# Delta stage in tiles of 64 tokens of two sequences, 64x64 blocks, and the decays in one matmul per eight heads

## The reference

```python
qkvz = x @ W_in                      # 128 -> 4 * 1024
b, a = jnp.split(x @ W_ba, 2, axis=-1)
qkv = silu(causal_conv_of_4_taps(qkv, conv_w))   # every channel for itself
beta = jax.nn.sigmoid(b)
g = -A * jax.nn.softplus(a + dt_bias)
q = _l2norm(q) * HD ** (-0.5)
k = _l2norm(k)
def step(S, inp):                    # over the tokens of one sequence
    qt, kt, vt, gt, bt = inp
    S = S * jnp.exp(gt)[..., None, None]
    pred = jnp.einsum('bhk,bhkv->bhv', kt, S)
    S = S + jnp.einsum('bhk,bhv->bhkv', kt, (vt - pred) * bt[..., None])
    o = jnp.einsum('bhk,bhkv->bhv', qt, S)
    return (S, o)
...
y = y * jax.lax.rsqrt(jnp.mean(y * y, axis=-1, keepdims=True) + 1e-06)
y = norm_w * y * jax.nn.silu(z)
return y.reshape(Bb, Tt, KV) @ W_o
```

## Time and profile before

| | |
|---|---|
| median of 3 runs | 6675.69 us (6673.12, 6675.69, 6717.01) |
| span of the profiled execution | 6691.0 us |
| delta loop, 16 turns | some 3890 us of it, from 125 us to some 4020 us |
| one tile, t = 0 and 2 / 1 / 3 | 57.7 / 62.5 / 64.5 us |
| busy over the span | PE 5879.5, DVE 3696.7, ACT 3292.2, POOL 2549.1 us |

### The profile page before, as it was taken

One profiled execution on the slowest core, in us unless ns is written; L12 is line 12 of the kernel. 1 busy time (PEld: TensorE's weight loads), 2 busy tenths in 40 slices (PEclk: granted clock), 3 DMA queues, 4 the chain that ended last, 5 costly groups with the idle time before them and its releaser, 6 DMA issues. The chain is left out here.

```text
span 6691.0 us, 188335 instructions
## 1 busy us (share of the span) xinstructions
PE 5879.5 (88%) x67493; PEld 4461.9 (67%) x67494; DVE 3696.7 (55%) x7182; ACT 3292.2 (49%) x7191; POOL 2549.1 (38%) x2432
## 2 busy tenths in 40 slices
PE   5999999999999999999999997668888799995586
PEld 4777777777777777777777775556666566664486
DVE  5555555555555555555555555654444466665443
ACT  2555555555555555555555552242333345552165
POOL 5545444544454545454544453340000200003553
PEclk9999999999999999999999997888898899996598
DMA  3000000000000000000000001020000000001124
GB/s 96 21 22 19 18 22 22 18 19 22 21 19 19 21 22 19 19 21 22 19 18 22 22 18 32 28 77 1 1 1 0 3 0 0 0 0 40 38 62 123
DMA packets 99365, 161.44 MB, mean 24 GB/s; under 512 B 19973, under 2 KB 82245, under 8 KB 96069
## 3 DMA queue, kind: packets, MB, share of 16 engines
q1 hardware_dynamic: 76260, 121.44, 6.0%
q0 software_dynamic: 14080, 26.64, 1.2%
q10 hardware_dynamic: 8320, 4.19, 0.2%
HBM read 118.03 MB, written 104.87 MB: 33 GB/s over the span
## 5 line engine op out<-in xcount | busy, mean ns | idle before, releaser
L802 PE MATMUL bank<-wc,hT 128*128 128x512 f32 (+1 forms) x2344 | 1077.6, 571 | 47.6 <-issue 29.0
L972 PE MATMUL bank<-X,kqe 128*128 128x64 f32 x6240 | 775.4, 278 | 42.1 <-DVE rb L1472 19.7
L972 PEld LDWEIGHTS bank<-X,kqe 128*128 128x128 f32 x6240 | 727.5, 192 | 84.1 <-DVE rb L1472 55.1
L1210 ACT ACTIVATE TT<-bank 128x512 bf16<-128x512 f32 x640 | 381.8, 597 | 612.8 <-PE bank L953 612.8
L1512 DVE TENSOR_TENSOR yb<-bank,masks 128x512 bf16<-128x512 f32 x768 | 526.5, 687 | 137.1 <-PE bank L935 135.8
L802 PEld LDWEIGHTS bank<-wc,hT 128*128 128x128 f32 x2344 | 391.0, 191 | 310.5 <-issue 282.2
L1310 POOL TENSOR_TENSOR qa<-qa,qt 128x512 f32<-128x512 f32 x390 | 487.4, 1271 | 34.8 <-POOL qt L1305 34.8
L1451 DVE TENSOR_TENSOR kqe<-bank,ex 128x512 f32<-128x512 f32 x520 | 335.1, 686 | 273.8 <-PE bank L879 273.8
L1210 ACT ACTIVATE T<-bank 128x512 bf16<-128x512 f32 x640 | 349.5, 595 | 272.1 <-PE bank L946 270.2
L1343 POOL TENSOR_SCALAR_AFFINE_SELECT kqe<-kqe 128x512 f32<-128x512 f32 x260 | 215.7, 830 | 641.0 <-DVE kqe L1451 640.9
L1305 POOL TENSOR_TENSOR qt<-qp,cq 128x512 f32<-128x512 f32 x390 | 400.4, 1048 | 28.0 <-POOL qa L1310 28.0
(11 more groups left out here) (536 smaller groups left out, 13459.3 us busy)
## 6 DMA issues: line engine op xcount, KB each, us to landing
sent_l0f<-blank_l0f SPq DMA_DIRECT2D x64, 528.0 KB
sent_l1m<-blank_l1m SPq DMA_DIRECT2D x64, 528.0 KB
xin<-sent_l1m SPq DMA_DIRECT2D x139, 66.0 KB
taken_l1m<-back_l1m SPq DMA_DIRECT2D x16, 512.0 KB, 8.7
xin<-sent_l0f SPq DMA_DIRECT2D x75, 66.0 KB
decay_sums<-decay_rows SPq DMA_DIRECT2D x264, 3.0 KB
cw_stage<-in_L_attn_conv_w_dram SPq DMA_DIRECT2D x4, 1024.0 KB, 6.3
out_dram<-x_sb ACTq DMA_DIRECT2D x8, 512.0 KB, 7.4
```

The costliest lines, as they stand in the source:

```text
L802: mm = pe.matmul(bk[:, cols], src[:, j:j + P], w["wc"][:, j, at * 512 + cols.start:at * 512 + cols.stop], start=(j == 0), stop=(j == TAPS ...
L972: mm = pe.matmul(bk[:, i * D0:(i + 1) * D0], lhsT(hh), rhs(hh), start=True, stop=True)
L1210: nc.scalar.activation(dst, bk[:, :].rearrange("p (h a u) -> p h a u", h=8, u=1 << l), ACT.Copy).then_inc(actb.done.sem, 1)
```

## The change

A tile now holds 64 tokens of each of two sequences, one on partitions 0 to 63 and one on 64 to 127. A loop turn is still four tiles, now four steps of the same two sequences of 256 tokens, and there are still 16 turns. All blocks within a tile are 64x64. So there are 6 levels, `products` runs twice with eight heads each (32 small matmuls in place of 16), r1, r3 and o multiply 64x64 blocks (`own_heads`), and the state is carried over three times in a turn: `state` and `from_state` are 64x64 too and stand in tiles 1, 2 and 3, and POOL scales the state (`state_past`). The decays of eight heads come from one bf16 matmul of 118 rows, which holds the mask, the sums and the bias; the exponential is one ACT instruction for eight heads. `hT` is written into four shifted copies (`shifted`). The input arrives in another order, and eight transfers in the first expert stage bring the rows back into the old order.

```diff
-LEVELS = 7
+LEVELS = 6
...
-                pe.matmul(bk[:, :], c["oneb"][at, :], sums[at, (t + 1) % TPB, :], start=True, stop=False,
-                          skip_group_check=True)
-                pe.matmul(bk[:, :].rearrange("p (h i) -> p h i", h=HB), c["identb"][:, :],
-                          c["hide"][:, :].unsqueeze(1).to_broadcast([P, HB, P]), start=False, stop=True,
-                          skip_group_check=True).then_inc(actb.full.sem, 1)
+                pe.matmul(bk[:, :], weights[0:ROWS, (t + 1) % TPB, :], sums[0:ROWS, (t + 1) % TPB, hb * 512:(hb + 1) * 512],
+                          start=True, stop=True).then_inc(actb.full.sem, 1)
 
             def products(b, hb):
 
                 banks = dveb.fill(pe, b, f"kq.{2 * hb}", banks=2)
-                for i in range(2):
-                    for two, bk in enumerate(banks):
-                        hh = hb * HB + two + 2 * i
-                        mm = pe.matmul(bk[:, i * 256:(i + 1) * 256], kqT[rows(hh), hh // 2, 0, :],
-                                       kqT[rows(hh), hh // 2, :, :].rearrange("p a n -> p (a n)"),
-                                       start=True, stop=True)
-                        if i == 1:
-                            mm.then_inc(dveb.full.sem, 1)
+                pe.sem_inc(pe_passed, 1)
+                for i in range(4):
+                    pr = 4 * hb + i
+                    for s in range(NB):
+                        for two, bk in enumerate(banks):
+                            mm = pe.matmul(bk[of(s), i * 2 * BS:(i + 1) * 2 * BS], kqT[rows(two), pr, 0, of(s)],
+                                           kqT[rows(two), pr, :, of(s)], start=True, stop=True)
+                            if i == 3 and s == NB - 1:
+                                mm.then_inc(dveb.full.sem, 1)
...
+            def own_heads(b, name, half, a, after=0):
+
+                bk = dveb.fill(pe, b, name, after)
+                pe.sem_inc(pe_passed, 1)
+                for i in range(8):
+                    hh = 2 * i + half
+                    for s in range(NB):
+                        mm = pe.matmul(bk[of(s), i * D0:(i + 1) * D0], a[of(s), hh, :], X[of(s), hh, :],
+                                       start=True, stop=True)
+                mm.then_inc(dveb.full.sem, 1)
...
+            def state(b, t):
+
                 dveb.was_done(pe, b, t, "r4.1")
-                if half == 0:
-                    pe.wait_ge(kd_ready.sem, kd_ready.at(b, t // 2 + 1))
-                bk = actb.fill(pe, b, f"s.{half}")
-                for i in range(8):
-                    hh = half * 8 + i
-                    mm = pe.matmul(bk[rows(hh), i // 2 * D0:(i // 2 + 1) * D0], kd[:, hh, :], X[:, hh, :],
-                                   start=True, stop=True)
-                mm.then_inc(actb.full.sem, 1)
+                pe.wait_ge(*kd_of(b, t - 1))
+                banks = dveb.fill(pe, b, "s.0", banks=NB)
+                pe.sem_inc(pe_passed, 1)
+                for hh in range(H0):
+                    for s, bk in enumerate(banks):
+                        mm = pe.matmul(bk[rows(hh), hh // 2 * D0:(hh // 2 + 1) * D0], kd[1 - t % 2][of(s), hh, :],
+                                       X[of(s), hh, :], start=True, stop=True)
+                        if hh == H0 - 1:
+                            mm.then_inc(dveb.full.sem, 1)
 
             def from_state(b, t, a, name):
 
-                for half in range(2):
-                    if a == 0:
-                        actb.was_done(pe, b, t, f"s.{half}")
-                    bk = dveb.fill(pe, b, f"{name}.{half}")
-                    for i in range(4):
-                        pr = half * 4 + i
-                        mm = pe.matmul(bk[:, i * P:(i + 1) * P], kqT[:, pr, a, :], S[:, pr, :], start=True, stop=True)
-                    mm.then_inc(dveb.full.sem, 1)
+                if a == 0:
+                    dveb.was_done(pe, b, t, "s.1")
+                banks = dveb.fill(pe, b, f"{name}.0", banks=2)
+                pe.sem_inc(pe_passed, 1)
+                for pr in range(PAIRS):
+                    for s in range(NB):
+                        for two, bk in enumerate(banks):
+                            mm = pe.matmul(bk[of(s), pr * D0:(pr + 1) * D0], kqT[rows(two), pr, a, of(s)],
+                                           S[rows(two), s, pr, :], start=True, stop=True)
+                            if pr == PAIRS - 1 and s == NB - 1:
+                                mm.then_inc(dveb.full.sem, 1)
...
-                            if l == 6:
-                                if t % 2 == 1:
-                                    state(b, t, G)
-                                if G == 0:
-                                    actb.was_done(pe, b, t, "h")
-                                taps(b, hT[t % 2], "k0", 2 * G, 2)
+                        if l == LEVELS - 1:
+                            if t > 0:
+                                state(b, t)
+                            actb.was_done(pe, b, t, "h")
+                            taps(b, shifted[t % 2], "k0", 0, 4)
...
-                        if l == 5:
-                            query_squares(b, t + 1)
+                    query_squares(b, t + 1)
                     turn_squares(b, t)
-                    if t % 2 == 1:
+                    if t > 0:
                         decay(b, t, 0)
                         decay(b, t, 1)
-                        taps(b, hT[t % 2], "k1", 0, 2)
+                        taps(b, shifted[t % 2], "k1", 0, 2)
                         from_state(b, t, 0, "ks")
                         from_state(b, t, 1, "qs")
                     decayed(b, t)
...
                 product(0)
                 product(1)
...
                 product(2)
                 product(3)
                 scale_z(b, t)
-                product(4)
-                product(5)
-                product(6)
-                product(7)
                 add_out(b, t)
...
+                            correct(b, t, step, G)
                             if (l, G) == (1, 0):
                                 sum_squares_k(b, t + 1)
-                            if (l, G) == (6, 1):
-                                squares_by_token(b, t + 1)
-                                sum_squares_o(b, t)
+                            if l == LEVELS - 1:
+                                silu(b, f"z{G}", z2)
...
+                    if t > 0:
+                        dve.wait_ge(S_ready.sem, S_ready.at(b, t - 1))
+                        for s in range(NB):
+                            bk = dveb.empty(dve, b, f"s.{s}")
+                            dve.tensor_tensor(S[:, s, :, :], S[:, s, :, :], bk[:, :].rearrange("p (k n) -> p k n", n=D0),
+                                              ALU.add).then_inc(dveb.done.sem, 1)
+                    squares_of_q(b)
+                    scale_k(b, t)
+                    squares_by_token(b, t + 1)
+                    sum_squares_o(b, t)
```

More of the change, by code:

```diff
@@ L22 @@
 TPB = 2
+NB = 2
+BS = P // NB
+STEPS = NB * TPB
 BIG = 1.0e30
@@ L522, in level_masks @@
+            dve.wait_ge(astep, A_GATES)
+            dec = gates["dec"][:, 0:tiles, :]
+            dve.tensor_tensor(dec, dec, beta[:, :, :], ALU.mult).then_inc(dstep, 1)
+            dve.wait_ge(dstep, D_ALL + 1)
 def level_masks(ctx, nc, c):
     HALF = P // 2
-    m0, compact, hide, one = c["mask0"], c["masks"], c["hide"], c["oneb"]
+    m0, compact = c["mask0"], c["masks"]
     m = ctx.enter_context(nc.sbuf_tensor("masks_whole", [P, LEVELS, P], BF16))
@@ L531, in gpsimd @@
         pool.memset(m[:, :, :], 0.0).then_inc(step, 1)
-        pool.memset(one[:, :], 1.0).then_inc(step, 1)
-        pool.memset(hide[:, :], 0.0).then_inc(step, 1)
-        pool.wait_ge(step, 3)
-        pool.affine_select(out=hide[:, :], in_=hide[:, :], compare_op=ALU.is_ge, fill=-BIG, base=0,
-                           pattern=[[1, P]], channel_multiplier=-1).then_inc(step, 1)
-        n = 4
+        pool.wait_ge(step, 1)
+        n = 1
         for l in range(LEVELS):
@@ L677, in delta_attention @@
         fs = sb("fs", [P, 3, H0])
-        kd = sb("kd", [P, H0, D0])
+        kd = [sb(f"kd{t}", [P, H0, D0]) for t in range(TPB)]
         sqT = sb("sqT", [P, PAIRS, P])
@@ new lines, in solve @@
+                    return
+                before = dveb.uses.at(t, {"r2": "r1", "r3": "r2", "r4": "r3", "o": "r4"}[step] + f".{half}")
+                if step in ("r2", "r4"):
+                    heads(dveb, b, f"{step}.{half}", half, lambda hh: TT[1 - t % 2][:, hh, :], lambda hh: rb[:, hh, :], before)
+                else:
+                    own_heads(b, f"{step}.{half}", half, k_part if step == "r3" else q_part, before)
+            def state(b, t):
+                dveb.was_done(pe, b, t, "r4.1")
+                pe.wait_ge(*kd_of(b, t - 1))
[7 more added lines that the diff above has]
+                            mm.then_inc(dveb.full.sem, 1)
@@ L1027, in _ @@
                 for t in range(U):
```

(21 more changed lines are left out.)

549 lines of the change are left out of this document (332 added, 217 removed).

## The result

The changed kernel takes 6526.13 us (median of 4 runs, 6521.78 to 6542.89) against 6675.59 (6673.12 to 6717.01): ratio 0.975, 95% interval 0.970 to 0.980. Its profiled run has a span of 6520.6 us against 6691.0. That is 170 us less in the spans and 149 us less in the medians, where I forecast 76: the direction and the wide range (6430 to 6790) held, the forecast's own range (6530 to 6670) was missed by 4 us, and the size was off by about a factor of two. On another chip the same kernel took 6527.69 us, ratio 0.975 (0.969 to 0.981).

The account below looks back on a forecast made before the run. PE was taken to bound the kernel, with waits through DVE and ACT returning part of the work removed. 6691 - 171 + 25 + 15 + 5 + 50 = 6615, median 6600 us; own range 6530 to 6670, wide 6430 to 6790.

Parts of the forecast that it names:

- extra instruction: Instruction holding a wait before each tiled group, 11 a tile: 0.4 us a tile taken, 25 us in all.
- the clock: PE clock in the loop: three more 1.8 us gaps a turn, 1.5 more slow tiles, 3.1 us a turn, 50 us.
- start: Before the loop: 32 input transfers in place of four and longer gate chains, 15 us taken from 10 to 30.
- expert stage, rest: Eight transfers on ACT's queue bringing rows back in the expert stage: 5 us taken from 0 to 30.
- What the waits give back: Step walking PE through a tile: some 22 of 33 us a turn return as waits, leaving 171 us gained.
- walk: PE followed through a tile with new durations: tile 0 takes 52.4 us, tiles 1 to 3 59.1 each.
- `products` to the next tile: Last stretch of a tile: work falls 3.3 us, waits return most; 13.1 us from 13.7, a gain of 0.6.
- Rival B: Loop clock at 0.95 costs 185 us in place of 50: 6735 us, no change by the bound; 18%.
- A: Rival: two corners writing one PSUM bank in r1, r3, o don't overlap, 76 ns a pass: 6980 us, slower; 15%.
- C: Rival: PE's order hides more, waits are shorter, half of what was given back stays: 6425 us, faster; 12%.
- the three waits that I named: PE waits: near 1.8 us on DVE before the state, 1.6 before the q product, 1 on ACT before `project_out`.
- D: Rival: longer chains, each of some twelve engine hand-overs a tile costs 0.15 us more, 115 us: 6715; 12%.

Follow-up runs that it names:

- corner: Changed kernel with r1, r3 and o issuing all passes of the first sequence before the second's instead of alternating; 6709.82 us (one run).
- y_first: Changed kernel with ACT evacuating both halves of y before its second turning of k to bf16; 6376.54 us, ratio to before 0.959.
- sem_twice: Changed kernel with the extra TensorE queue instruction ahead of each tiled group issued twice; 6605.25 us, ratio to before 0.988.
- all3: Changed kernel with taps_first, y_first and ks_taps together; 6289.31 us, ratio to before 0.941.
- all5: all3 with, in place of taps_first's order, DVE making both z behind the second mask of step o, in state tiles only; 6252.47 us, ratio 0.939.
- all6: all3 with the two decay matmuls issued ahead of `turn_squares`; 6258.15 us, ratio to before 0.939.
- ks_taps: Changed kernel with the product of k with the state issued before the two k1 taps; 6488.68 us, ratio to before 0.970.
- taps_first: Changed kernel with the four k0 taps issued before the state product; 6449.55 us, ratio to before 0.969.

## Why the prediction was right or wrong

**Direction and mechanism: right.** PE bounds the tile, the work taken off it counts, and a large part comes back as round trips through DVE and ACT. PE lost 571 us of busy time (forecast 530) and the span fell by 170.

**The terms of the sum.**

| term | forecast | measured |
|---|---|---|
| turns of the loop, extra instruction included | -171 + 25 | -205 |
| the clock | +50 | +22 |
| start | +15 | +19 |
| expert stage, rest | +5 | +1 |
| last solve behind the loop | not in the sum | -7 |
| sum | -76 | -170 (170.4 in the spans, 149 in the medians) |

The profiled execution of the kernel before lay 15 us above its median and that of the changed kernel 6 us below, which is the difference between the last two numbers. The +1 of the rest is not a measurement of that stage, since it varies by 53 us between runs.

The failed step is "What the waits give back", with the price of the extra instruction: 59 of the 94 us that were missing, 34 in the walk alone and up to 25 in the instruction, the whole if its price is nothing. The mechanism was right, and the terms were mis-sized. "Tile 0 then takes 52.4 us, tiles 1 to 3 59.1 each" and 0.4 more for the instruction; they take 52.2 and 58.45. Against my walk of a state tile, without that 0.4:

- Level 1 takes 4.83 us (998.48 to 1003.31; walk 5.2), level 3 4.77 (1006.62 to 1011.39; 5.1), level 5 to `products` 22.53 in an undisturbed tile (1076.12 to 1098.65; 23.0). The groups were priced from too far a row: r1, r3 and o 1.08 us (1.22), `products` 1.03 (1.13), state and its products 1.09 each (1.22 each), the two decay matmuls 0.44 (0.55). corner shows for r1, r3 and o that such a difference passes to some 80% into the tile. The sum of the small ones is 1.5 us of work a state tile and 1.15 in tile 0, 92 us in the loop; at 80% for all of them some 73 us of time (an estimate). It is the largest error, and the next one hid half of it.
- `products` to the next tile takes 13.7 us (1040.23 to 1053.93), as before, where I had 13.1. That is 0.6 us a tile, 38 us, the other way. The wait for ACT is 1.87, not 1.1, while the one before `turn_y` is 0.63, not 1.0: for ACT I counted the turning of k on ACT, and not all of the time that it stands for POOL behind DVE. y_first shows that the order on ACT is the whole cause, and that it costs 1.9 us in each of 64 tiles, 107 us of the loop. This is the largest part of what was "given back", and the easiest to have back.
- The instruction ahead of each tiled group: forecast 0.4 us a tile. The one round trip that both kernels have says 0.01 where it counts; sem_twice says that another one would cost 0.8. The price of the first stays open.

**The clock.** The other 28 us. I took 3.1 us a turn; it is 22 us in 16 turns, 1.4 a turn. The rate was read from one tile of 66.54 us and a guess of how many turns have such a one. A spell looks as forecast: it begins right behind a gap. In the tile above, the k0 taps behind the 1.73 us take 5.40 us, and the next tile's take 3.70 behind the same wait. The windows of the two, with the granted clock third from the end:

```profile
1022.57:1025.00 2.43, 2.43 (x10) 1.08 (x4) 1.28 (x2) 0.00 (x0) 1.88 (x1) 0.53 0.00 0
1025.00:1027.80 2.80, 2.80 (x6) 1.03 (x5) 0.00 (x0) 0.00 (x0) 0.00 (x0) 0.80 0.00 0
1082.69:1086.30 3.61, 3.61 (x18) 1.60 (x12) 1.28 (x2) 0.00 (x0) 1.88 (x1) 1.00 0.02 5
```

0.53 is near the lower of the two levels, 1.2 GHz in place of 2.4. One spell costs 5.40 - 3.70 = 1.7 us (a tile of 60.10 in place of 58.45), not the 2.07 that I read from the earlier trace rows, and there are fewer of them: 17 of the 63 distances lie more than 1.2 us above their kind, against 6 before, where 1.5 more a turn made 24. In both kernels the tile with the jump has the most (9 of the 17, and all 6); the other 8 are in tiles that had none before. The kernels that have removed the gaps above 1 us inside the tile (all3, all5, all6) lose 4 to 14 us to spells in the loop, most of it in tile 3 with the jump; those that still have at least two such gaps 22 to 56. Within the latter the number doesn't follow the gaps: ks_taps has one gap fewer than the changed kernel and loses 17 us more. What decides there isn't settled. Rival B at 0.95 was far off: the loop's windows show 0.99 and 1.00.

**The rest.** The start costs 19 us for 15. SP takes twice as long for the input as in the earlier trace rows:

```profile
2.49 21.66 SPq L168 DMA_DIRECT2D x_sb<-in_L_attn_x_dram  x32
```

11.5 of the 19 us are there; that these and the longer gate chains are the cause is argued from the trace, and no experiment tested it. The last solve was missing from my sum: its three corner steps take 2.08 us each for both halves, where they took 3.68, 3.79 and 5.03.

**The rivals.** A is refuted by corner. The Trainium skill (TensorEngine Tiling, "Gotcha 1: PSUM Pressure") says that different row tiles cannot use one PSUM bank at the same time; here two of them do, on different partitions, with starts 30 ns apart where one corner alone has 54. C, shorter waits, is the direction in which the result lies, but for another reason: the three waits that I named were as long as I walked, to 0.1 us, or longer, and the work was cheaper. D didn't show: the hand-over in level 3 took 0.95 us for 0.94.

**Small matmuls.** The state's 64 passes take 1.09 us, 17 ns each, in this kernel too (1021.48 to 1022.57). The Trainium skill (TensorE: Matmul & The Clock Gate, "Wait — 56ns, not 53.3ns?") has starts never nearer than about 25 ns; here, with four corners in turn, they are nearer, and the measurement decides.

## What to carry to other kernels

When work leaves the bounding engine, walk the order of every engine that feeds it: a copy that was two places from its waiter can now stand behind another engine's chain, and moving three lines (all3) was worth 238 us, more than the change itself. A gap fills as far as the work put into it doesn't need what the gap waits for: 1.9 us of 1.87 in y_first, 1.15 of 1.60 in ks_taps, and 0.8 of 1.73 in taps_first, where the taps need a bank of the same chain. Inside one chain, as in all6, it only moves. Before small terms are summed, price them from the nearest row and ask in which direction each is off: here all the small groups were off the same way, by some 0.1 us in a dozen places of each tile.

## What was not expected of the hardware

- A second instruction of PE's queue that only raises a semaphore costs nothing behind most other work and 0.15 us behind a wait (sem_twice).
- Two corners of the array that write different partitions of one PSUM bank overlap: 30 ns from pass to pass in place of 54 (corner).
- Ahead of a corner group that waits for nothing, PE's starts are 0.33 us apart in place of 0.24: `join_tt` at 1016.25, o at 1016.58. With the semaphore instruction doubled it is the same 0.33 (1032.35 to 1032.68), so those 0.09 us aren't that instruction; the kernel before, which has none, shows 0.32 ahead of its state group (1107.29 to 1107.61). What they are is open.
- A part of the program that no edit touched differed by up to 53 us between profiled runs (2640 to 2693), as much as most of the edits were worth.
